# Latents' attention on one Trainium2 core: VectorE's read of the side products moved between the weighted values and the norm

## The reference, cut to what matters

```python
attn = softmax(A1) - lam * softmax(A2)          # causal, 16 heads of 8
O = einsum('bhnm,bhmd->bhnd', attn, V)          # 16 values a head
rms = jnp.sqrt(jnp.mean(O * O, axis=-1, keepdims=True) + EPS)
O = O / rms * rms_scale * (1.0 - LAMBDA_INIT)
x = x + O.transpose(0, 2, 1, 3).reshape(b, n, H * 2 * dh) @ Wo.T
logits = einsum('bsd,ed->bse', layernorm(x), gate_w) + gate_b
```

## Time and profile before

| | |
|---|---|
| median of 3 runs | 950.28 us |
| lowest and highest | 945.99 and 950.51 us |
| the profiled execution | 948.75 us, span 946.9 us |
| TensorE busy | 912.1 us, 96% of the span |
| VectorE busy | 797.4 us, 84% |
| ScalarE busy | 701.4 us, 74% |
| POOL busy | 378.1 us, 40% |

### The profile page before, as it was taken

One profiled execution on the slowest core, in us unless ns is written; L12 is line 12 of the kernel. 1 busy time (PEld: TensorE's weight loads), 2 busy tenths in 40 slices (PEclk: granted clock), 3 DMA queues, 4 the chain that ended last, 5 costly groups with the idle time before them and its releaser, 6 DMA issues.

```text
span 946.9 us, 20546 instructions
## 1 busy us (share of the span) xinstructions
PE 912.1 (96%) x8268; PEld 492.4 (52%) x8268; DVE 797.4 (84%) x1591; ACT 701.4 (74%) x1003; POOL 378.1 (40%) x378
## 2 busy tenths in 40 slices
PE   8679999999999999999999999999999999999997
PEld 5444444545454545454545454545454545556763
DVE  5979797979798989888888888888889696588987
ACT  4756869787878787878787969697878766855644
POOL 6473034343434343434343434343434230426345
PEclk9879999999999999999999999999999999999999
DMA  6403030303030303030303030303020200000000
GB/s 214 84 1 72 1 94 1 93 3 73 23 72 23 73 24 73 23 73 23 73 23 74 23 72 23 74 23 73 23 60 23 39 23 2 23 24 24 2 2 23
DMA packets 74566, 41.96 MB, mean 44 GB/s; under 512 B 62276, under 2 KB 69864, under 8 KB 74472
## 3 DMA queue, kind: packets, MB, share of 16 engines
q1 hardware_dynamic: 74184, 39.60, 17.0%
q10 hardware_dynamic: 288, 1.05, 0.3%
HBM read 25.98 MB, written 0.59 MB: 28 GB/s over the span
## 4 chain that ended last, share of the span: by engine, by line
PE 81%; DVE 13%; ACT 3%; issue 2%; DMA 1%; POOL 0%; DVEq 0%; ACTq 0%
PE S L2158 10%; PE S L2149 9%; PE OA L2182 9%; PE OA L2185 9%; PE OA L2188 9%; PE S L2152 9%; PE WW L2092 9%; PE WW L2119 1%; PE WW L2121 1%; DVE amx L803 1%; PE WW L2120 1%; PE WW L2079 1%; PE WW L2081 1%; PE WW L2080 1%; DVE mx L1517 1%
## 5 line engine op out<-in xcount | busy, mean ns | idle before, releaser
L1866 ACT ACTIVATE region<-S,sigma 128x1024 f16<-128x1024 f32 x208 | 231.5, 1113 | 135.0 <-PE S L2158 134.9
L1546 DVE TENSOR_TENSOR region<-S,region 128x1024 f16<-128x1024 f32 x208 | 252.3, 1213 | 42.8 <-ACT S L1870 42.7
L1534 DVE TENSOR_REDUCE mx<-WW 128x1 f32<-128x512 f32 (+1 forms) x480 | 262.6, 583 | 29.8 <-PE WW L2092 22.6
L1870 ACT ACTIVATE S<-S,sigma 128x1024 f32<-128x1024 f32 x208 | 224.3, 1078 | 0.0
L1678 POOL TENSOR_TENSOR xk<-raw,xk 128x508 f16<-128x508 f32 x64 | 63.2, 997 | 169.6 <-DVE xk L1413 169.6
L2092 PE MATMUL WW<-xT,region 128*128 128x512 f16 x360 | 124.8, 381 | 3.4 <-DVE region L1525 2.1
L2149 PE MATMUL S<-region,xT 128*128 128x512 f16 (+1 forms) x416 | 124.5, 380 | 3.2 <-DVE region L1546 2.6
L2182 PE MATMUL OA<-region,xk 128*128 128x512 f16 (+1 forms) x416 | 123.8, 379 | 0.0
L2152 PE MATMUL S<-region,xT 128*128 128x512 f16 (+1 forms) x416 | 123.7, 379 | 0.0
L2158 PE MATMUL S<-region,xT 128*128 128x512 f16 (+1 forms) x416 | 123.7, 379 | 0.0
L2185 PE MATMUL OA<-region,xk 128*128 128x512 f16 (+1 forms) x416 | 123.7, 379 | 0.0
(11 more groups left out here) (318 smaller groups left out, 1836.2 us busy)
## 6 DMA issues: line engine op xcount, KB each, us to landing
raw<-ctx SPq DMA_DIRECT2D x16, 768.0 KB
rb<-inv_dram SPq DMA_DIRECT2D x16, 512.0 KB, 3.7
xT<-xk SPq DMA_TRANSPOSE x48, 3.2
left_row<-left_pT SPq DMA_DIRECT2D x48, 2.0 KB
raw<-ctx SPq DMA_DIRECT2D x16, 32.5 KB
WO_lo<-L_xattn_Wq ACTq DMA_DIRECT2D x1, 512.0 KB, 4.0
WO_hi<-L_xattn_Wkv ACTq DMA_DIRECT2D x1, 512.0 KB, 4.8
lx<-x SPq DMA_DIRECT2D x1, 512.0 KB, 7.3
```

What stands on the lines that cost most here:

```text
L1534: nc.vector.tensor_reduce(mx[:, r, c:c + 1], W[BANK[("m", n)]][:, 0:width], AX.X, ALU.max)\
L1546: nc.vector.tensor_tensor(p_lo[k], src, p_hi[k], ALU.subtract).then_inc(lo_done.sem, 1)
L1866: nc.scalar.activation(p_hi[k], src, ACT.Exp, scale=sigma[:, 0:1])
L1870: nc.scalar.activation(src, src, ACT.Exp, scale=sigma[:, 0:1]).then_inc(e_done.sem, 1)
```

## The change

The first half of `side_reads` (the wait for `side1`, L850, L853, L855) becomes `side_taken`, the second half `side_statistics`. `combine` takes a number n, and where it is given, calls `side_taken(n)` behind L820 and ahead of the wait for `t12` and L826. The loop gives it from turn 2 to turn 7 and calls only `side_statistics` behind `combine`. The three reads behind the loop still call both halves in one.

```diff
--- before.py
+++ after.py
@@ -808,7 +808,7 @@
                                         src, bc(amx[:, 16 * k:16 * k + 16], 64), ALU.subtract)\
                   .then_inc(ta["shifted"].sem, 1)
 
-            def combine(t):
+            def combine(t, n=None):
                 wait(dve, "pv", t)
                 pv = WW[:, :, 0:16 * VW].rearrange("p c (k d) -> p c k d", d=VW)
                 nc.vector.reciprocal(arc[:], pv[:, :, :, 2 * SD]).then_inc(ta["r"].sem, 1)
@@ -819,6 +819,8 @@
                 wait(dve, "r2", t)
                 nc.vector.tensor_tensor(t12[:], pv[:, :, :, 0:2 * SD], bc(arc[:], 2 * SD), ALU.mult)\
                   .then_inc(ta["t12"].sem, 1)
+                if n is not None:
+                    side_taken(n)
                 wait(dve, "t12", t)
                 if not first(t):
                     wait(dve, "oc", t.plus(-1))
@@ -842,7 +844,7 @@
                                         Ob[:].rearrange("p (h d) -> p h d", h=SH), bc(oms[:, 2, :], 2 * SD),
                                         ALU.mult).then_inc(ta["oc"].sem, 1)
 
-            def side_reads(n):
+            def side_taken(n):
 
                 wait(dve, "side1", side(n))
                 if n <= TB:
@@ -855,11 +857,17 @@
                     ins = nc.vector.tensor_tensor(lg[:, 0, t, :], OA[:, 1, 128 + NE * k:128 + NE * k + NE], gbias[:],
                                                   ALU.add)
                 ins.then_inc(ta["side1_out"].sem, 1)
+
+            def side_statistics(n):
                 wait(dve, "side1_out", side(n))
                 if n <= TB:
                     ln_statistics(link, n - 1)
                 if n == X1_SIDE:
                     ln_statistics(link, TB)
+
+            def side_reads(n):
+                side_taken(n)
+                side_statistics(n)
 
             def gating(g):
 
@@ -918,9 +926,9 @@
             for m in range(TB):
                 t = Turn(m)
                 if m > 0:
-                    combine(t.plus(-1))
+                    combine(t.plus(-1), m - 1 if m > 1 else None)
                 if m > 1:
-                    side_reads(m - 1)
+                    side_statistics(m - 1)
                 if m + 1 < TB:
                     maxima(t.plus(1), 0)
                 if m + 2 < TB:
```

## The result

The changed kernel takes 953.13 us (median of 6 runs, 951.37 to 954.27) against 948.84 for the kernel before (6 runs, 945.99 to 950.51): by the medians 4.3 us more. The measured ratio is 1.0054, with a 95% interval from 1.0039 to 1.0069, which is 5.1 us; how it weighs the runs is not given. The medians of these twelve runs make 1.0045, and so do their means; that too is inside the interval. So the changed kernel is slower, by 0.4 to 0.7%. The profiled execution has a span of 950.8 us.

What follows compares the result with a forecast made beforehand. TensorE carries 81% of the chain of waits, VectorE 13%, including the changed part. Turns 2 to 7 add 0.1 + 1.35 + 1.25 + 1.27 + 1.18 + 0.3 = 5.4 us to 950.28: 955.7 us, range 951.0 to 958.0.

Steps and rivals of the forecast that it cites:

- rival (b): Delay partly taken up as ScalarE and TensorE run ahead: 2.9 us slower, 953.2 us; chance 0.20.
- its line of 0.5%: Whole kernel: 4.75 us, about what a measurement can tell from no change; slower given 0.56, the same 0.40, faster 0.04.
- the signs that it named: Turns 4 to 6: read idle 1.3 to 1.5, L814 to L674 4.3 to 4.7; turn 3 idle some 2.7.
- Turns 4 and 5: Side products arrive 2.75 and 2.66 after L814, so VectorE waits: turn 4 grows by 1.25 us, turn 5 by 1.27.
- The saving of 0.23 by parting dependent pairs: VectorE, each turn: new order separates dependent instructions, 1.21 to 0.98 us, if the products were there at once.
- Turn 6: Products come 2.57 after L814, so VectorE idles 1.4 ahead of the read and the turn grows by 1.18 us.
- L674 4.34: VectorE in turn 6: the statistics L674 start 4.34 us after L814, where today it is 3.16.
- Turn 7: Products at 1.8 after L814, POOL's power exposed, TensorE's wait gone: net +0.3 us, low end -0.3.
- Its premise that TensorE's lead does not grow: Turn 7: turn 6's late L807 holds ScalarE's exponential and copies, so products come 1.8 after L814.
- Turns 2 and 3: Turn 2 grows 0.1 us near POOL's subtractions; turn 3 grows 1.35 as the norm comes behind the wait.
- Rival (a): Turn 2: Ob is caught behind POOL's subtractions, 1.17 us instead of 0.1; 6.5 us slower, 956.8; chance 0.15.
- Rival (c): Turns 4 to 7: products come before 1.2 after L814, six turns save 0.23 each; 948.9 us; chance 0.10.

Runs made afterwards that it cites:

- e9: The changed kernel unedited, run again for a second profile: 951.87 us against 946.80 for the kernel before, ratio 1.0054.
- e4: The new order in turns 4 to 6 alone, the old one elsewhere: 952.00 us against 947.24 for the kernel before, ratio 1.0052.
- e5: The changed kernel with ScalarE's copies and TensorE's side products moved earlier in turns 4 to 7 (short trip); executed once, turns 2 to 7 sum to 66.9 us.
- e6: The kernel before with the side products read between the sum over squares and L834's scaling in turns 4 to 6; executed once, turns sum to 64.0 us.
- e3: The new order in turn 7 alone, the old one elsewhere; executed once, turn 7 takes 7.51 us against 7.21 in the kernel before.
- e2: The new order in turns 3 to 7, the old one in turn 2; executed once, turns sum to 67.9 us against 62.8 before.
- e1: The new order in turn 2 alone, the old one elsewhere; executed once, turns 2 and 3 take 24.70 us against 24.77 before.
- e7: The kernel before with e5's short trip and the side products read right behind Ob in turns 4 to 6: 948.56 us, ratio 1.0006.
- e11: The changed kernel unedited, executed once more for a third profile: turn 3 takes 12.55 us, turns 2 to 7 sum to 67.8.

## Why the prediction was right, point by point

It was right in sign and mechanism, and near in size: 5.4 us forecast, 5.0 in the turns without a fall, 5.1 by the ratio, 4.3 by the medians. Its absolute time, 955.7, is 2.6 over the measured 953.13, and outside its own likeliest stretch of 954.5 to 957; 1.4 of this is the median that it counted from, 950.28 from three runs, which is 948.84 from six. The measured time is in fact that of rival (b), 953.2, by chance: it is the turns that tell the two apart. And 0.54%, with an interval from 0.39 to 0.69, does not settle on which side of its line of 0.5% the change lies.

Of the signs that it named, the read's idle time in turns 4 to 6 is 1.35, 1.41 and 1.24, in turn 3 2.42 without the fall (e9), L814 to L674 takes 4.56, 4.43 and 4.25, and turn 7's wait for TensorE's values is gone. By term:

| turn | forecast | measured (e9 less before) |
|---|---|---|
| 2 | +0.1 | +0.26 |
| 3 | +1.35 | +0.99 |
| 4 | +1.25 | +1.18 |
| 5 | +1.27 | +1.25 |
| 6 | +1.18 | +1.39 |
| 7 | +0.3 | -0.04 |
| sum | 5.4 | 5.0 |

**Turns 4 and 5** came out to 0.1, and e4 and e5 show both sides of it: the order in these turns alone costs 3.95 with turn 6, and a short trip takes turn 4 back to 11.40. In turn 4 the 0.15 that a late turn 3 gives back is there too: 12.68 in e4, 12.53 behind a late turn 3.

**The saving of 0.23 by parting dependent pairs** is in the timeline: L857 is 0.15 long and Ob starts 0.07 behind its start. Of it only 0.08 was collected, in e6's turn 5; elsewhere the products or POOL came first.

**Turn 6** was undersized by 0.2. The step "L674 4.34" came out at 4.25 (907.71 - 903.46), 0.09 less; what the term left out is POOL. L836 ends 1.50 later in the turn than L834 did (907.81 - 903.46 = 4.35 against 903.73 - 900.88 = 2.85), and with 2.91 for the power Oc starts at 7.37 after L814, 0.12 later than behind L674 alone. L685 then waits for POOL's L680 and starts 0.51 after Oc, where it was 0.33: 0.18 more. 1.09 + 0.12 + 0.18 is the 1.39 of the table. The prediction saw this exposure in turn 7 and not in turn 6, which has no keys either.

**Turn 7** was oversized by 0.3. The products came 1.51 after L814 (915.50 - 913.99) and not 1.8. Its premise that TensorE's lead does not grow was wrong: POOL holds VectorE up behind the L807 that lets ScalarE and TensorE go on in turn 6 (from that L807 to the next L814 it is now 4.42, and was 4.12), and TensorE's transposes start 0.50 ahead of L814 and not 0.14. e3, whose turn 6 is as before, has 0.16, and its products come 1.86 after L814. Oc starts 6.45 after L814 and not 6.72. The whole term, -0.04, lies midway between 0.3 and its low end.

**Turns 2 and 3** are 1.25 together against 1.45, since the two terms do not add: turn 3 alone has its 1.35 (1.32 in e2), but what turn 2 loses on VectorE comes off turn 3's wait. Rival (a), Ob caught behind POOL, did not happen. Both start at once, and Ob runs its usual length:

```profile
854.28 0.41 DVE L828 TENSOR_TENSOR Ob<-t 128x256 f32<-128x256 f32 x1
854.73 1.27 DVE L831 TENSOR_TENSOR Osq<-Ob 128x256 f32<-128x256 f32 x1
```

```profile
854.29 4.96 POOL L550 TENSOR_TENSOR ew<-region,o_hi 128x512 f16<-128x512 f32 x4 [1.17 <-ACT o_hi L1855]
```

```profile
862.14 0.43 DVE L843 TENSOR_TENSOR Oc<-Ob,oms 128x256 f32<-128x256 f32 x1 [0.97 <-POOL oms L981]
```

POOL's four subtractions took 4.96 and not 4.69, so POOL was the one held: they take 4.95 or 4.96 in all six profiles with the new order in turn 2, and 4.68 or 4.69 in the other seven. Its power came later, 7.37 after L814 and not 7.11, and Oc with it: turn 2's 0.26. The products of turn 3 did not come later by it (in e9 they end 17.14 after turn 2's L814, before 17.22), so turn 3 gave it back; e1 shows both halves.

**Rival (b)**, half of the delay taken up, is contradicted by e4. A little of it is true: 0.15 in turn 4, and what turn 7 does not lose. **Rival (c)** needed the products at 1.2 after L814; e5 brought them to between 1.4 and 1.9, and no turn 4 to 6 got shorter than before by it.

## What to carry to other kernels

Before an instruction that waits is moved forward, find when what it waits for arrives, on the clock of its own turn, and count what stood in front of it as cover: here four instructions of 1.5 us on VectorE hid a trip through ScalarE and TensorE that began at VectorE's own preceding subtraction, and turns 3 to 6 paid for their loss, 1.0 to 1.4 us each. Where the trip starts from the reader's own engine, being late does not help the reader: turns 5 and 6 grew as much in e4 as in the changed kernel. Compare kernels by the lengths of their turns in the trace, which repeat to 0.02 us outside the falls of the clock, when the spans of single executions scatter by several.

## What was not expected of the hardware

A fall of TensorE's granted clock from 2.4 to 1.2 GHz, 3 to 4 us long, came at one of two places in the loop in 7 of the 13 profiles and at none in the other 6, and in unedited kernels came and went from one execution to the next; it cost 0.26 to 1.53 us, by whether TensorE was the bound there. Falls lie in the first 60 us of every profile too, of different lengths, and most of the scatter of single spans goes with them: in four profiles (before, e1, e7, e11) the clock is at 0.50 up to 58 us or beyond, and there L751 of VectorE starts at 63.3 to 63.7; in the other nine at 60.3 to 62.0. Where VectorE and POOL started within 0.01 us of each other on SBUF operands, VectorE kept its 0.41 and POOL's group of four grew from 4.69 to 4.96; the VectorE instruction behind it, 0.45 later, took 1.27 where 0.42 is usual. GpSimd's power of 128x16 values takes 2.9 us, and 0.54 for 128x1, and VectorE waited for it in turns 2, 6 and 7.
